# A two-layer decoder on one core: the recurrence's numerator as a ScalarE scaling and a GpSimd addition in place of one VectorE pass

## The reference

```python
w = -jnp.exp(time_decay); u = time_first
...
def step(carry, kv_t):
    aa, bb, pp = carry
    kt, vt = kv_t
    ww = u + kt
    q = jnp.maximum(pp, ww)
    e1 = jnp.exp(pp - q)
    e2 = jnp.exp(ww - q)
    y_t = (e1 * aa + e2 * vt) / (e1 * bb + e2)
    ww2 = pp + w
    q2 = jnp.maximum(ww2, kt)
    e1b = jnp.exp(ww2 - q2)
    e2b = jnp.exp(kt - q2)
    return (e1b * aa + e2b * vt, e1b * bb + e2b, q2), y_t
```

## Time and profile before

| what | us |
| --- | --- |
| median of 3 runs | 2637.64 |
| lowest and highest run | 2634.35, 2638.93 |
| the profiled execution, whole | 2634.15 |
| its span, first to last instruction | 2632.2 |
| busy in the span: TensorE (matmuls) | 2009.7 (76%) |
| VectorE | 1850.9 (70%) |
| ScalarE | 1297.3 (49%) |
| GpSimd | 945.4 (36%) |
| the recurrence, from L814 to the last pass of L878 | 477.2 to 573.6 |

### The profile page before, as it was taken

The page is one execution under the profiler, slowest core; times in us unless marked ns, Lnnn a source line. Parts: engine busy times, 40 slices in busy tenths (PEclk is TensorE's granted clock), DMA queues, the critical chain, the costliest instruction groups (busy, mean ns, idle before and its releaser), DMA issues. The chain is left out here.

```text
span 2632.2 us, 33369 instructions
## 1 busy us (share of the span) xinstructions
PE 2009.7 (76%) x12104; PEld 1245.7 (47%) x12139; DVE 1850.9 (70%) x2514; ACT 1297.3 (49%) x2147; POOL 945.4 (36%) x547
## 2 busy tenths in 40 slices
PE   2888765025499999999956799988994776699985
PEld 1456642012376666666633566753542332244442
DVE  4249984986777888888843465554443997999976
ACT  0013322655386776776713232325554875466656
POOL 1014443213246777877725222224101000444330
PEclk8988877557699999999988899998997898899998
DMA  3225655001538999999951000002335330000001
GB/s 145 64 102 189 219 199 221 0 0 33 194 111 265 265 276 271 259 271 277 255 144 63 1 1 1 1 27 102 96 96 181 133 111 1 0 1 1 0 1 64
DMA packets 119668, 305.52 MB, mean 116 GB/s; under 512 B 29521, under 2 KB 49489, under 8 KB 115794
## 3 DMA queue, kind: packets, MB, share of 16 engines
q1 hardware_dynamic: 98450, 252.58, 26.3%
q0 software_dynamic: 21056, 50.84, 10.1%
HBM read 215.67 MB, written 88.77 MB: 116 GB/s over the span
## 5 line engine op out<-in xcount | busy, mean ns | idle before, releaser
L1330 PE MATMUL x_group<-x_xt,x_gu 128*128 128x256 f16 x2640 | 362.0, 275 | 33.4 <-DVE x_part L1441 17.9
L1441 DVE SCALAR_TENSOR_TENSOR x_part<-x_group,x_scale,x_part 128x256 f32<-128x256 f32 x660 | 286.5, 474 | 94.9 <-ACT x_part L1383 84.0
L1296 POOL TENSOR_TENSOR x_part<-x_part 128x512 f32<-128x512 f32 x165 | 236.0, 1430 | 169.5 <-DVE x_part L1441 168.7
L1330 PEld LDWEIGHTS x_group<-x_xt,x_gu 128*128 128x128 fp8e4 x2640 | 229.4, 98 | 140.6 <-issue 60.0
L1383 ACT ACTIVATE x_part<-x_group,x_scale 128x256 f32<-128x256 f32 x660 | 264.5, 472 | 10.8 <-PE x_group L1330 10.6
L2440 POOL TENSOR_TENSOR f_part<-f_part 128x1024 f32<-128x1024 f32 x44 | 120.5, 2738 | 187.6 <-DVE f_part L2467 187.6
L158 PE MATMUL mean_n<-residual,const_tables 128*128 128x512 f32 x160 | 78.7, 647 | 139.8 <-PEq L765 104.1
L1776 POOL TENSOR_TENSOR c_pt<-c_pt,const_tables 128x1024 f32<-128x1024 f32 x32 | 75.8, 2369 | 255.7 <-ACT c_pt L1750 255.7
L2338 PE MATMUL f_group<-f_x_hi,f_raw 128*128 128x512 f16 x352 | 138.7, 394 | 33.0 <-DVE f_part L2467 25.7
L1287 POOL DMA_INDIRECT mixed_rows<-x_y,moe_rows x94 | 150.1, 1597 | 32.0 <-issue 20.1
L1347 PE MATMUL x_y_ps<-x_d_hi,x_h_hi 128*128 128x512 f32 x330 | 157.8, 478 | 2.7 <-ACT x_y L1405 1.8
(11 more groups left out here) (332 smaller groups left out, 4993.2 us busy)
## 6 DMA issues: line engine op xcount, KB each, us to landing
x_d_hi<-down_hi SPq DMA_DIRECT2D x50, 768.0 KB
x_d_lo<-down_lo SPq DMA_DIRECT2D x50, 768.0 KB
x_gu<-codes_gu SPq DMA_DIRECT2D x50, 384.0 KB
p_w<-d_s SPq DMA_DIRECT2D x17, 768.0 KB, 7.7
down_hi<-p_hi SPq DMA_DIRECT2D x17, 768.0 KB, 3.9
down_lo<-p_lo SPq DMA_DIRECT2D x17, 768.0 KB, 6.3
aux<-ct SPq DMA_DIRECT2D x2, 4096.0 KB, 15.3
cross_values<-y_v_out SPq DMA_DIRECT2D x16, 512.0 KB, 2.8
```

The lines of the kernel that those rows point to most:

```text
L1296: pool.tensor_tensor(x[:, 0, :, :], x[:, 0, :, :], x[:, 1, :, :], ALU.add).then_inc(summed, 1)
L1330: mm = pe.matmul(group_ps[s % 2][:, q, :], codes[:, q, col:col + P], xt[u][:, k, q, :], start=k == 0, stop=k == 1)
L1441: dve.scalar_tensor_tensor(x, group_ps[s % 2][:, 2 + q, :], scale[v][:, o, 2 + q:3 + q], x, ALU.mult, ALU.add).then_inc(ev_dve, 1)
```

## The change

The numerator is no longer a pass of VectorE. ScalarE gets a new step `weigh(n)`, behind `invert(n)`: a Copy with a scale per partition, in place on `kv`, that waits for the second scan of piece n and increments the new semaphore `weighted`. GpSimd gets `numerator(n)`: it waits for `weighted` and adds `aa`, one token earlier, in place. GpSimd's order becomes: product of piece n, numerator of piece n-1; after the loop the numerator of piece 7. No buffer is added, and no transfer is touched.

```diff
@@ -802,6 +802,12 @@
                 act.activation(v, v, ACT.Copy, scale=V_GAIN).then_inc(e_ready, 1)
+
+            def weigh(n):
+                c = n // (B // BP)
+                x = kv[n % RING_E][:, :, 1:S]
+                act.wait_ge(scanned, 2 * n + 2)
+                act.activation(x, x, ACT.Copy, scale=e_first[:, c:c + 1]).then_inc(weighted, 1)
 
             def invert(n):
...
                 invert(n)
+                weigh(n)
 
         @block.gpsimd
         def _(pool):
+            def numerator(n):
+                x = kv[n % RING_E][:, :, 1:S]
+                pool.wait_ge(weighted, n + 1)
+                pool.tensor_tensor(x, x, aa[n % 2][:, :, 0:S - 1], ALU.add).then_inc(num_ready, 1)
+
...
                 pool.tensor_tensor(kv[n % RING_E][:, :, :], e[n % RING_E][:, :, :], v, ALU.mult).then_inc(kv_ready, 1)
+                if n >= 1:
+                    numerator(n - 1)
+            numerator(PIECES - 1)
 
         @block.vector
...
-
-            def numerator(n):
-                c = n // (B // BP)
-                x = kv[n % RING_E][:, :, 1:S]
-                dve.wait_ge(scanned, 2 * n + 2)
-                dve.scalar_tensor_tensor(x, x, e_first[:, c:c + 1], aa[n % 2][:, :, 0:S - 1], ALU.mult, ALU.add)\
-                   .then_inc(num_ready, 1)
...
                 if n >= 1:
                     finish(n - 1)
-                numerator(n)
             finish(PIECES - 1)
```

More of the change, by code:

```diff
@@ L779, in wkv @@
         (shift_ready, decay_exp, held, first_exp, fade_ready, zeroed, fades_ready, e_ready, kv_ready, scanned, den_ready,
-         num_ready, logged, inverted, product, done, step_sem) = (
+         num_ready, weighted, logged, inverted, product, done, step_sem) = (
             sem(n) for n in ("shift_ready", "decay_exp", "held", "first_exp", "fade_ready", "zeroed", "fades_ready",
-                             "e_ready", "kv_ready", "scanned", "den_ready", "num_ready", "logged", "inverted", "product",
+                             "e_ready", "kv_ready", "scanned", "den_ready", "num_ready", "weighted", "logged", "inverted", "product",
                              "done", "step"))
```

## The result

The changed kernel takes 2645.94 us (median of 5 runs, 2645.29 to 2648.49), the kernel before 2635.17 (5 runs, 2634.16 to 2638.93): a ratio of 1.004, with a 95% interval of 1.0029 to 1.0052. It is slower by 10.8 us where 9.7 were forecast. The profiled execution has a span of 2644.1 us.

The account below looks back on a forecast made before the run. VectorE plus GpSimd bound the recurrence, 9.13 + 2.10 = 11.23 us a round, their passes excluding each other. Terms -0.2 + 4.5 + 2.1 + 3.3 = +9.7 us on the 2637.64 median gave 2647 us, range 2641 to 2653.

Parts of the forecast that it names:

- start, to piece 2's first scan: Start of the recurrence: piece 2's denominator scan begins at 505.4 where it began at 505.56, a gain of 0.2 us.
- five rounds: Pieces 2 to 6: each round takes 12.14 us, 0.91 more than before, together +4.5 us.
- piece 7, to its denominator's end: Last piece: no GpSimd product is left, but numerator 6's addition is, +2.1 us.
- end, to the last pass's end: After the last denominator: uncovered chain of inversion, copy, GpSimd addition and closing passes, 9.6 us against 6.26, +3.3.
- The price of an addition: VectorE time lost to each GpSimd addition in the loop: taken as 2.10 us, like the product.
- the alternative weighed beside that row: VectorE blocked for GpSimd's whole instruction: 0.29 us more for each of seven additions, sum +11.7; no chance given.
- ScalarE's copy: Scaling of the numerator on ScalarE after the inversion: 1.1 us, hidden in rounds 2 to 6.
- an addition beside VectorE: Rival: GpSimd's addition runs beside VectorE's passes, rounds of 10.04 us, sum -3.4, 2634 us; chance 6%.
- a dear addition: Rival: rows of 255 stream worse on GpSimd; +14.2 us at 2.74 each, +24 at 4.2; chance 10%.
- late numerators: Rival: scaled numerators reach the closing passes too late; each us beyond costs 5 us over the rounds; chance 3%.
- Piece 7's addition: Late variant: GpSimd gets numerator 6 only after piece 7's denominator, during ScalarE's inversion; sum +7.6, 2645 us; chance 12%.
- TensorE's first matmul: Sign of being right: the first matmul after the stage comes near 583.6, its wait near 114 us.

Follow-up runs that it names:

- the fifth run: The changed kernel with the decay tile in PSUM in place of SBUF, against the kernel before: 2622.27 us against 2637.67, ratio 0.9943.

## Why the prediction was right

Its terms, read again from the two timelines, against what it said:

| term | forecast | measured | from |
| --- | --- | --- | --- |
| start, to piece 2's first scan | -0.2 | 0.0 | 489.09 to 507.02, 17.93 us; before 487.64 to 505.56, 17.92 |
| five rounds | +4.5 | +4.3 | 60.50 against 56.19 |
| piece 7, to its denominator's end | +2.1 | +2.05 | 567.52 to 575.12, 7.60; before 5.55 |
| end, to the last pass's end | +3.3 | +3.3 | 575.12 to 584.69, 9.57; before 6.26 |
| sum | +9.7 | +9.67 | TensorE's wait: 113.79 against 104.12 |

The step that carried it is that VectorE's 4.36 us for a scan were not its own: 2.10 of them were GpSimd's. That was read from the trace of before and is shown now from three sides: with a fill on GpSimd that reads nothing, with one operand of VectorE in PSUM, and with the work brought home to VectorE. The price of an addition, the one unknown, came out at 12.10 - 7.94 - 2.10 = 2.06 us (a measured round, less VectorE's own passes, less the product), close to the product's; 4 runs of 255 cost GpSimd nothing extra (2.33 us where it ran alone). Had the addition cost its whole length, 2.39, the alternative weighed beside that row, rounds would be 12.14 + 0.29 = 12.43; none was over 12.13. ScalarE's copy took 1.13 us where 1.1 was taken, and no table load came in with it (16 in the stage before and after).

The rivals: an addition beside VectorE was excluded by the lengthened passes; a dear addition by 2.33 alone and 2.06 in a round; late numerators by the two waits, neither of them in rounds 2 to 6. Piece 7's addition did not come late: GpSimd got numerator 6 during its denominator (571.91, 3.29 us), ahead of the inversion.

The median moved by 10.8 us and the stage by 9.67. The interval of the ratio, 7.6 to 13.7 us, holds both, and the rest is not assigned. TensorE's first matmul came at 585.01 and not near 583.6, since its wait began 1.46 us later in this execution (471.22 for 469.76); in the six experiments, whose code ahead of the stage is the same, it began between 470.01 and 472.07, so that is scatter. That 2645.94 lies so near to 2647 is in part luck: with two more runs the median before fell from 2637.64 to 2635.17, and the change was 1.1 us larger than the sum.

## What to carry to other kernels

Before moving work from VectorE to GpSimd, look at the pairs of instructions that would lie side by side: where VectorE's pass has both operands in SBUF and GpSimd's reads SBUF, their times add up (here the addition cost VectorE 2.06 us for a pass of 1.19 taken off it), and an engine's busy share hides it, since the wait counts as busy. Passes with one operand can be caught too, as the last section shows. A pass that is longer in the timeline than its twin elsewhere is the sign. Three ways out paid here: the work brought back to VectorE (1.15 us a round for 2.10), one operand in PSUM, and the GpSimd instruction timed beside passes that have one there.

## What was not expected

- A scan with its decay operand in PSUM takes as long as from SBUF: 2.26 to 2.29 us for 128x1024 in both.
- A fill by GpSimd, which left the two-operand passes alone, held back a small VectorE pass with one operand: the pass over 128x4 ahead of the loop takes 3.53 us beside the fill of 128x4096 (3.51 us), in the kernel before as after, and 0.17 us where that fill is gone. Which property of that pass makes it wait was not tried.
- The alternating rounds of 8.3 and 10.1 us in the fifth run: a steady order of instructions need not give a steady round.
- Two operands in SBUF are not the only case. The four passes that add the decay to its tile ahead of the loop read one tile, yet beside GpSimd's first two products they take 6.88 us in all, where they take 2.73 without (shortest, median and longest of the four in ns, kernel before). That is 4.15 more, 2.08 a product. With the tile in PSUM all four take 1.27 us each, and the two products keep their plain length (4.65 us together).

```profile
L885 DVE TENSOR_SCALAR w_fades<-w_fades,w_fade x4: 740/1776/2824, 480.7 to 486.9; 128x1020 f32<-128x1020 f32 x4
```
